# A fused attention and FFN kernel on one core: three small steps of the FFN and of the next batch move later in a token loop

## What is computed

```python
x = x + layernorm(attention(layernorm(x), w_qkv, w_proj))
x = x + layernorm(ffn(layernorm(x), ...))
# attention, 16 heads of 16 channels, 64 landmarks (means over 16 tokens):
kernel1 = softmax(Q @ K_l.T)          # 1024 x 64 a head
kernel2 = softmax(Q_l @ K_l.T)        # 64 x 64
kernel3 = softmax(Q_l @ K.T)          # 64 x 1024
SV  = (kernel1 @ iterative_inv(kernel2)) @ (kernel3 @ V)
out = SV @ w_proj
# ffn, 8 experts: one expert for the whole batch, by reconstruction loss
h      = relu(x @ Wd1[e] + bd1[e])
loss_e = mean((h @ Wd2[e] + bd2[e] - x) ** 2);  idx = argmin(loss)
out    = x @ W_base + b_base + relu(x @ Wa_down[idx] + ba_down[idx]) @ Wa_up[idx] + ba_up[idx]
```

## Time and profile before

| what | value |
|---|---|
| median of three runs | 2231.13 us (2229.5 to 2233.48) |
| the profiled execution's own time | 2235.6 us |
| its span, first to last instruction | 2233.9 us |
| PE busy | 2022.2 us, 91% |
| PEld busy | 1314.7 us, 59% |
| DVE busy | 1442.4 us, 65% |
| ACT busy | 864.7 us, 39% |
| POOL busy | 700.7 us, 31% |
| TensorE's granted clock, mean over the span | 0.971 |
| chain of work that ended last, by engine | PE 57%, DVE 20%, SP's queue 8%, issue 5%, ACT 4%, POOL 3% |
| its two largest lines | L991 11%, L1199 11% |

### The profile page before, as it was taken

One profiled execution on the slowest core, in us unless ns is written; L12 is line 12 of the kernel. 1 busy time (PEld: TensorE's weight loads), 2 busy tenths in 40 slices (PEclk: granted clock), 3 DMA queues, 4 the chain that ended last, 5 costly groups with the idle time before them and its releaser, 6 DMA issues.

```text
span 2233.9 us, 59429 instructions
## 1 busy us (share of the span) xinstructions
PE 2022.2 (91%) x25341; PEld 1314.7 (59%) x25341; DVE 1442.4 (65%) x3303; ACT 864.7 (39%) x1509; POOL 700.7 (31%) x918
## 2 busy tenths in 40 slices
PE   4889999999999999999999998999999999999955
PEld 2655757566574756657475564757657475665724
DVE  4667575776757676675766767576675757767541
ACT  3344344343434434343344434334343443434320
POOL 4152142422315232332523223252231524223052
PEclk9999999999999999999999999999999999999977
DMA  6213151331414123152422315132231513313020
GB/s 156 49 53 70 30 131 33 88 64 31 115 30 125 39 79 66 20 134 30 117 47 71 67 28 133 31 103 51 67 78 31 129 34 86 68 36 91 12 57 19
DMA packets 232974, 150.74 MB, mean 67 GB/s; under 512 B 153035, under 2 KB 203732, under 8 KB 232693
## 3 DMA queue, kind: packets, MB, share of 16 engines
q1 hardware_dynamic: 232710, 146.95, 28.1%
HBM read 36.98 MB, written 16.78 MB: 24 GB/s over the span
## 4 chain that ended last, share of the span: by engine, by line
PE 57%; DVE 20%; SPq 8%; issue 5%; ACT 4%; POOL 3%; DMA 2%; DVEq 1%; POOLq 0%; ACTq 0%
PE NS L991 11%; PE ringF L1199 11%; SPq L432 8%; PE ringA L1158 5%; PE ringF L1184 5%; PE ringA L885 4%; DVE mx L1560 3%; PE ringF L1232 3%; DVE mx L1546 3%; DVE stage L1634 3%; PE KV L1072 2%; PE ringF L885 2%; PE ringA L1058 2%; PE ringA L1034 2%; PE ringF L1234 2%
## 5 line engine op out<-in xcount | busy, mean ns | idle before, releaser
L1199 PE MATMUL ringF<-x,H 128*128 128x256 f16 x1536 | 237.9, 273 | 0.0
L1560 DVE TENSOR_REDUCE mx<-ringA 128x8 f32<-128x512 f32 x256 | 175.4, 686 | 91.0 <-PE ringA L1034 89.9
L687 ACT ACTIVATE E<-ringA,score_scale 128x512 f32<-128x512 f32 x256 | 175.5, 686 | 132.7 <-PE ringA L1058 132.6
L1199 PE MATMUL ringF<-H 128*128 128x128 f16 x1024 | 204.4, 220 | 1.4 <-DVE H L1645 1.4
L521 POOL TENSOR_SCALAR vtmp<-mv,eps_ffn 128x8 f32<-128x8 f32 x16 | 5.1, 316 | 606.6 <-DVE mv L1391 606.6
L1611 DVE SCALAR_TENSOR_TENSOR X<-X,NS 128x320 f32<-128x320 f32 x160 | 78.0, 488 | 179.1 <-PE NS L991 173.9
L885 PE MATMUL ringA<-xT,wqkv 128*128 128x512 f16 x768 | 176.5, 379 | 17.8 <-ACT QS L705 11.7
L1184 PE MATMUL ringF<-wd,x2T 128*128 128x512 f16 x768 | 185.4, 380 | 3.4 <-DVE H L1645 3.2
L695 ACT ACTIVATE E<-ringA,score_scale 128x512 f32<-128x512 f32 x256 | 158.6, 685 | 73.4 <-PE ringA L1089 73.4
L1546 DVE TENSOR_REDUCE mx<-ringA 128x1 f32<-128x512 f32 x256 | 160.1, 682 | 30.1 <-PE ringA L1025 30.1
L521 POOL TENSOR_SCALAR vtmp<-mv,eps_ln 128x8 f32<-128x8 f32 x32 | 9.9, 310 | 506.1 <-DVE mv L1391 506.1
(11 more groups left out here) (262 smaller groups left out, 4277.1 us busy)
## 6 DMA issues: line engine op xcount, KB each, us to landing
KS<-stage SPq DMA_DIRECT2D x384, 64.0 KB, 2.0
QS<-stage SPq DMA_DIRECT2D x384, 64.0 KB, 2.0
xin<-in_L_attn_x_dram SPq DMA_DIRECT2D x16, 1024.0 KB, 10.9
xres<-in_L_attn_x_dram SPq DMA_DIRECT2D x16, 1024.0 KB, 8.0
out_dram<-yout SPq DMA_DIRECT2D x16, 1024.0 KB, 5.5
QS<-LB SPq DMA_DIRECT2D x16, 512.0 KB, 4.4
E<-in_L_attn_w_qkv_dram SPq DMA_DIRECT2D x1, 768.0 KB, 7.0
H<-in_L_ffn_Wd_dram SPq DMA_DIRECT2D x2, 256.0 KB
```

Source lines behind the costliest of these rows:

```text
L687: A(E[:, k % ESLOTS, :], ps[:, :], ACT.Exp, scale=score_scale[:, 0:1]).then_inc(freed["s3"].sem, 1)
L1199: ins = MM(dst, H[:, a, t, own], src, start=first and i == 0, stop=last and i >= 3, skip_group_check=True)
L1560: V_.reduce_max(mx1[:, t, 8 * h:8 * h + 8], take(b, "m1", k)[:, :].rearrange("p (a m) -> p a m", a=8), AX.X)\
```

## The change

In `body` of TensorE and of ScalarE the hidden tile 7 follows step 8 where it followed step 7. On VectorE its remainder follows `maxima1(b, 9)` where it followed `maxima1(b, 8)`; `aggregate(b + 1, 0)` follows step 10 where it followed step 8; `sum_of_squares(b - 1)` follows step 12 where it followed step 9. No instruction is added or removed.

```diff
@@ ScalarE, body @@
-                    if ffn and k in (1, 3, 5, 7):
-                        hidden(b - 1, 4 + k // 2)
+                    if ffn and k in (1, 3, 5, 8):
+                        hidden(b - 1, 4 + (1, 3, 5, 8).index(k))
@@ TensorE, body @@
-                    if ffn_too and k in (1, 3, 5, 7):
-                        hidden(b - 1, 4 + k // 2)
+                    if ffn_too and k in (1, 3, 5, 8):
+                        hidden(b - 1, 4 + (1, 3, 5, 8).index(k))
@@ VectorE, body @@
-                    if ffn and k in (2, 4, 6, 8):
-                        hidden(b - 1, 3 + k // 2)
+                    if ffn and k in (2, 4, 6, 9):
+                        hidden(b - 1, 4 + (2, 4, 6, 9).index(k))
                     if k == 2:
                         kernel2_normalise(b)
                     if more and k in (1, 3, 5, 7):
                         token_statistics(b + 1, 0, xin, x_in, T, range(k - 1, k + 1))
-                    if more and k == 8:
-                        aggregate(b + 1, 0)
                     if k == 8:
                         denominator_sums(b)
-                    if ffn and k == 9:
+                    if more and k == 10:
+                        aggregate(b + 1, 0)
+                    if ffn and k == 12:
                         sum_of_squares(b - 1)
```

## The result

The changed kernel takes 2192.98 us (median of four runs, 2190.85 to 2196.74). The kernel before takes 2232.31 us on the same chip (four runs, 2229.5 to 2235.63). The ratio is 0.9828 with an interval of 0.9809 to 0.9848: **39.3 us less**, where 33.6 had been forecast. A later job timed both again: 2194.62 us for the changed kernel, a ratio of 0.984 [0.9811, 0.987].

The account below looks back on a forecast made before the run. TensorE's computing plus its waits was taken to bound the kernel. Waits of 18 us and clock falls of 17.5 make 35.5; 2231.1 - 35.5 + 2 = 2197.6, rounded to 2197.5 us, range 2190 to 2214.

Parts of the forecast that it names:

- What bounds: Whole kernel: TensorE, busy 91%, sets the time; L1058's scores idle 35.4 us in sum for VectorE's maxima.
- the replay of the ring: Batch 7, steps 7 to 13, with old durations: step 10's 1.23 us wait goes, step 13 starts 1.2 us earlier.
- The waits, 18 us: Third softmax's loop: 17 us from 14 batches, 0.8 in batch 15, 0.3 in batch 0.
- The falls, 17.5 us: Behind step 10's wait: nine drops of TensorE's clock to 1.2 GHz vanish, 1.95 us each.
- The offset, 2 us: Whole kernel: half the 4.5 us between profiled execution and median, added to the forecast.
- What becomes late: Aggregate and GpSimd's normalised half come later, nearly 8 us of cover left; `gram` needs the remainder only behind the loop.
- Falls that stay: Loop: the 1.2 us are gained but the clock still drops in nine batches or elsewhere; 2213 us, chance 0.2.
- Nothing arrives: Behind or ahead of the loop: TensorE waits the gain away at the next place; 2231 us, chance 0.05.
- Slower: Steps 9 to 12: TensorE idles, the clock falls in all 14 batches at 3.4 us; 2243 us, chance 0.03.

Follow-up runs that it names:

- one filler: Kernel before, with one unread product of 512 columns (0.22 us) on TensorE in the wait of step 10; 2212.31 us, ratio 0.9913.
- the further spreading: Changed kernel with kernel2's normalisation, statistics, aggregate, squares, `first_iterate` and `ns_linear` moved to later steps, squares behind step 15; 2180.9 us, ratio 0.9773.
- wait put back: Changed kernel with four more unread sums on VectorE between the maxima of steps 8 and 9; 2247.26 us, ratio 1.0053.
- squares-only kernel: Kernel before with only the squares moved, from behind step 9 to behind step 12; 2216.44 us, ratio 0.9928.
- three fillers elsewhere: Kernel before with three unread products of 512 columns (0.65 us a batch) ahead of the loop, loop untouched; 2242.52 us, ratio 1.0041.
- squares only, one filler elsewhere: Kernel before with the squares moved behind step 12 and one unread product (0.22 us) ahead of the loop; 2216.89 us, ratio 0.9921.
- statistics and squares: Kernel before with only the next batch's aggregate (behind step 10) and the squares (behind step 12) moved; 2203.97 us, ratio 0.9862.
- hidden tile: Kernel before with only the last hidden tile moved, behind step 8 (VectorE's part behind the maxima of 9); 2202.08 us, ratio 0.9853.
- five fillers: Kernel before, with five unread products of 512 columns (1.08 us) on TensorE in the wait of step 10; 2218.3 us, ratio 0.9931.
- the two that spread further: Changed kernel with more VectorE work moved to later steps: squares behind step 15, 2180.9 us; squares back behind step 12, 2176.46 us.

## Why the prediction was right

**What bounds, and the replay of the ring.** Right. Every step of the replay came out within 0.05 us: no wait at step 10, gaps of about 0.17 and 0.19 us at steps 11 and 12 (forecast 0.14 and 0.2), step 13 at 7.84 us (7.8), the 0.35 us of step 15 unchanged. `first_iterate` did not wait.

**The waits, 18 us.** Right for the 14 batches: 1.21 us each, 17 us. Batch 15 got 0.75 for the interval before its L1006, where 0.8 was given. The 0.3 us for batch 0 can't be tested, since batch 0 differs by more than that between executions.

**The falls, 17.5 us.** All nine went, and with the wait in place one filler took them away too, so they did hang on TensorE's idle time there. The price of 1.95 us each was right within what can be measured (2.0 to 2.1). The count was low by one: ten falls were in the 13 intervals and all ten are gone, so 19.6 to 21.2 us and not 17.5. The filler experiments measure the falls apart from the wait, 14.5 and 18.1 us.

That the tenth fall, near L1025, is gone is most likely luck. All eleven such falls in the thirteen profiles came within 1.6 us of a wait of 1.8 us or more at L1025, and six waits of that size had none. This wait differs from batch to batch and from execution to execution of the same code. In batch 10 of the changed kernel, where the earlier trace rows has 2.18 us, it was

```profile
1344.84 0.39 PE L1025 MATMUL ringA<-KS,QlB 96*128 96x512 f16 x1 [1.34 <-DVE stage L1495]
```

and nowhere from batch 1 to 15 of that profile was it over 1.6 us. A batch with a fall here is longer by the wait as well as by the clock: the 2.1 us of the tenth are the price of both.

**The offset, 2 us.** The sum was made against the profiled execution and half its distance to the median added. On the profiled executions the difference is 41.1 and on the medians 39.3, against 35.5 forecast. The excess over the sum is 3.8 us on the medians; with the 2 us left out and the medians of the same job (2232.31) used, the forecast would have been 2196.8. What was missing was the tenth fall, 2.1 us, and up to 1.6 us by which the batches without a fall became shorter than the replay says; the rest is batch 0 and the tail.

**What becomes late.** Right, with one size off. GpSimd's half in `xtmp` (L539) ended at 994.57 and ScalarE asked for it at 1001.88, 7.3 us of cover where nearly 8 was forecast. The stretch itself had lengthened, see below. `gram` doesn't wait for the remainder.

**The rivals.** *Falls that stay* (2213) is out: 15 loops without a fall, and none behind a loop in either part of the change alone. The rule of the Trainium skill (TensorE: Matmul & The Clock Gate, "Why this matters for your kernels"), by which the clock drops in mid-kernel after gaps clearly longer than these, was given as a reason for this rival. These runs don't bear it out for this kind of stretch: a wait of 1.23 us with a fall behind nine of 14, one of 1.51 with a fall behind 13 of 14, and one filler product of 0.22 us that took them all away. That the 1.23 us had no fall behind any of 14 loops with the squares moved and a filler ahead shows that no length of a wait alone decides. Here the measurement decides. *Nothing arrives* is out for the change, but the further spreading showed its mechanism, 0.46 us given back behind the loop. *Slower* is out; its mechanism, a wait long enough that the clock falls in nearly every batch, is what the experiment with the wait put back shows, at 1.0053 of the time before.

**What was underrated** is how narrow the edge is. The prediction put each fall down to the wait of 1.23 us and called waits of 0.2 us harmless. The squares-only kernel has the 1.23 us whole and three falls instead of nine, and with one filler elsewhere none. Over all kernels, by what TensorE idled in steps 10 and 11 of a batch, in us:

| idle at steps 10, 11 | falls behind the loops of batches 1 to 14 | kernel |
|---|---|---|
| 1.51 and 0.2 | 13 of 14 | wait put back |
| 1.23 and 0.2 | 11 of 14 | three fillers elsewhere |
| 1.23 and 0.2 | 9 of 14 | before |
| 1.23 | 3 of 14 | squares only |
| 1.23 | 0 of 14 | squares only, one filler elsewhere |
| 1.01 and 0.2 | 0 of 14 | one filler |
| 0.70 | 0 of 14 | statistics and squares |
| 0.67 at step 11 | 0 of 14 | hidden tile |
| 0.2 at step 11 | 0 of 14 | five fillers |
| 0.2 at step 11 | 0 of 14 | the change (twice), the two that spread further |

Each row is one profiled execution, and the number of falls varies from one to the next, as the spread of the times shows (2206 to 2227 us for the squares alone). What stays open is the rule by which the clock is taken back: the runs show on which side of the edge a kernel lies, not what is counted, and not why one batch has a fall and the next has none.

## What to carry to other kernels

Replay the ring of buffers with the durations of the old trace: where three side jobs stand between two reads that free a buffer and none between the next, moving them to one a step is worth what the replay says, and the place to put them is where their engine waits anyway, not the loop's end. Read the granted clock behind every wait of about a microsecond that stands among small products, since such a wait may cost twice, 1.2 us by itself and 2 us by the clock here. A gain from clock falls can be had only once, so two edits that both remove them must not be added up.

## What was unexpected of the hardware

- **With an idle time of 1.23 us among small products the clock fell in 9 of 14 batches, and one product of 0.22 us was enough to keep it**: 2230.38 to 2212.31 us by a product whose result is unread, with 1.01 us of the wait left. The same 1.23 us without the 0.2 us behind it had three falls, and none with one filler elsewhere.
- **The kernel before varies with what the clock does**: 2216.5 to 2242.0 us over 38 executions of one code, with a mean granted clock of 0.982 in the shortest and 0.966 in the longest. The changed kernel, with no falls between batch 0 and the tail in either profile, took 2190.9 to 2196.7 us in its eight.
- **GpSimd's normalisation slowed down beside VectorE.** Four instructions of L539 took 2.71 us in the changed kernel, 2.16 before. They now run beside VectorE's G (L1591, two inputs from SBUF, 0.68 us), L1542 and the surrounding maxima:

```profile
991.86 2.71 POOL L539 TENSOR_SCALAR xtmp<-xin,rstd,nmr 128x256 f32<-128x256 f32 x4 [0.30 <-POOL nmr L533]
```

```profile
993.54 0.68 DVE L1591 SCALAR_TENSOR_TENSOR G<-X,eye_ns 128x512 f32<-128x512 f32 x1
```

  The other traces say which of these it is. Over the loops of batches 1 to 15 in all thirteen profiles, the four instructions took 2.64 to 2.79 us, summed one by one, in each of the 59 in which G ran wholly beside them. They took 2.21 to 2.29 in the 136 others, and in 12 of those L1542 ran wholly and G for 0.2 to 0.3 us beside them. So the slower ones go with G, by about 0.5 us, and not with L1542 or the maxima. What the two share is not shown. It cost nothing here, as it lies within the cover.

One correction to the description of the kernel before: the wait in `maxima3` (L1025) stands at its sixth group, and what releases it is VectorE's remainder (L1495), which frees the PSUM bank and itself comes behind the stacking DMA.
